# Spreading dt over the state partitions by DMA instead of by matmul, in stage 1 of a four-stage model

## The chip, the cores and the metric

The kernel runs on one core of a Trainium2 chip. The metric is the device time of one execution in microseconds; lower is better.

## What is computed

The input x has shape (2, 64, 64, 64) in float32. Four blocks are applied to it one after the other, each as `x = x + block(groupnorm(x))`. The first is a small graph and attention block, the third and fourth are Mamba2 blocks. The second, here called stage 1, is a selective state space block, and only it is changed. For each of 128 sequences of 64 steps, with 128 inner channels and 16 states for each channel, it computes (cut down from the reference):

```python
u  = silu(conv(x_in) + b_conv)
dt = softplus((u @ W_xproj[:4].T) @ W_dt.T + b_dt)
A  = -exp(A_log)
def step(h, (dt_t, B_t, C_t, u_t)):
    h = h * exp(dt_t[..., None] * A) + dt_t[..., None] * B_t[:, None, :] * u_t[..., None]
    y = einsum('bds,bs->bd', h, C_t)
```

Afterwards come y + u * D, a gate silu(z), the output projection and a layer norm.

## The kernel before

**Blocks and slots.** Stage 1 works through 16 blocks (`NK1`), each of 8 sequences of 64 steps, which is 512 columns. A tile has 128 partitions (inner channels) by 512 columns of float32, 256 KB. The recurrence needs channels times states, 2048 rows, so each block is cut into 16 slots (`S1`): slot s handles eight channels with all their 16 states, on 128 partitions. `channels_of(t)` gives the quarter q = s % 4 and the part r = s // 4, and the eight channels are the partitions 32q + 8r to 32q + 8r + 7 of the tile. There are 256 slots over the stage, counted by t.

**One slot.** Five steps follow each other, each on its own engine.

1. TensorE (`spread`, L539) copies the eight rows of dt (tile `dt1`) over the 128 partitions by a matmul with a 0/1 matrix, into PSUM bank 2 or 3. It does the same with the eight rows of dt * u (tile `dtu`) into bank 4, 5 or 6. Each is one float32 matmul from 32 rows, which appears in the trace as two weight loads and two matmuls. The two spreads of one turn of the loop lie in different quarters of the array.
2. ScalarE (L893) computes exp(dt * A) from the dt bank into one of three tiles `decay1`.
3. VectorE (`weigh`, L1345) multiplies the bank of dt * u by B, in place.
4. VectorE (`scan`, L1354) runs the recurrence over the columns into one of four tiles `hs`.
5. GpSimd (L1088) multiplies the result by C into one of eight tiles `hc`. After each four slots, TensorE (L564) gathers them back to channels in bank 7.

**The order.** Each engine runs a program written out by hand, slot by slot, in order, with waits on semaphores. In turn t TensorE spreads dt for slot t + 3, once the exponential of slot t + 1 is done, and dt * u for slot t + 2, once the scan of slot t - 1 is done; then it gathers, then it does its share of `front`. ScalarE computes the exponential of slot t + 2 once the scan of slot t - 1 is done. VectorE weighs slot t + 1 and scans slot t.

**The front.** While the slots of block k run, all engines prepare block k + 1 in small steps tied to the slot number (`front(s, f)`): the input projection in bank 0 (s = 0), u (s = 1), B and C (s = 2, 3), dt before the softplus in bank 0 and z in bank 1 (s = 3), the softplus (s = 5 to 11), and dt * u (s = 12). In the softplus ScalarE computes e = exp(-|v|) and the inverse of 2 + e into `inv1` (L867), VectorE multiplies them (L1338), and GpSimd adds the last term at L1065, which makes dt ("final"), and multiplies by u at L1070 ("ready"). Per block GpSimd does 16 multiplications for the slots and seven for the front and the gate.

**SyncE.** Its queue issues the kernel's loads at the start. From the end of stage 1 on it issues, for each of the eight later calls, transfers from SBUF to SBUF (`rows_of_x`, L358 and L359, from 64 partitions to 64), stores of 128 partitions to device memory (L363) and loads of rows into few partitions (`decay_rows` L253, `decay_cols` L261, the latter into three partitions at a time). During stage 1 it issues nothing.

Of the kernel before, what the change touches and what calls it, by code (L numbers as in the profile page):

```python
# [13 lines left out]
ALU = mybir.AluOpType  # L14
ACT = mybir.ActivationFunctionType
# [62 lines left out]
def program(nc, x, consts, pool_sel, state_sel, l0w, l1w, callw, out):  # L78
    ctx = ExitStack()
    with ctx:  # L80
# [220 lines left out]

            return (u - 3) % 8 in (7, 0, 3)

        U_BANKS, T_BANKS = (4, 5, 6), (2, 3)

        PARTS = {"s1_x_parts": ("tanh_x", "half_x", "gate_x"),
                 "s1_z_parts": ("tanh_z", "z_copied", "gate_z"),
# [27 lines left out]
        @block.sync  # L335
        def _(sp):
            sp.dma_start(cst, consts).then_inc(sg("constants_loaded"), 16)
            for b in range(NB):
                sp.dma_start(Otok[:, :, b, :], x_tok[b].rearrange("(t p) c -> p t c", p=128)).then_inc(
                    sg("x_loaded"), 16)  # L340
            sp.dma_start(w0, l0w).then_inc(sg("stage0_weights_loaded"), 16)
            sp.dma_start(poolS, pool_sel).then_inc(sg("stage0_weights_loaded"), 16)
            sp.dma_start(w1, l1w).then_inc(sg("stage1_weights_loaded"), 16)
            sp.dma_start(stateS, state_sel).then_inc(sg("stage1_weights_loaded"), 16)
            for d in range(2):
                sp.dma_start(raws[d], callw[d]).then_inc(sg(f"block_weights_loaded{d}"), 16)

            def call(m, n, d, c):

                def rows_of_x(g):  # L350
                    sp.wait_ge(sg("normed"), c * 8 + g + 1)
                    if g >= 2:
                        sp.wait_ge(sg("x_projected"), c * 16 + 2 * (g - 1))
                        sp.wait_ge(sg("bc_projected"), c * 8 + g - 1)
                    a = SEQS * g
                    for b in range(NB):
                        own, dst = XP[64 * b:64 * b + 64, :], XS[g % 2][b]
                        sp.dma_start(dst[0:64, :], own[:, a + 1:a + 1 + SEQS]).then_inc(sg(f"x_rows{g % 2}"), 16)  # L358
                        sp.dma_start(dst[64:128, :], own[:, a:a + SEQS]).then_inc(sg(f"x_rows{g % 2}"), 16)  # L359

                def keep(name):
                    sp.wait_ge(sg(f"split_{name}"), c + 1)
                    sp.dma_start(kept[NAMES.index(name)].rearrange("(p j) n -> p (j n)", j=3), SPLITS[name]).then_inc(  # L363
                        sg(f"stored_{name}"), 16)

                def rows_of_decay(g):
                    if g >= 2:
                        sp.wait_ge(sg("decay_logs"), c * L + 8 * (g - 1))
                    decay_rows(sp, g, 0, "M")
                    decay_cols(sp, g, 0, "M")  # L370
                    decay_cols(sp, g, 1, "G")
                    decay_rows(sp, g, 1, "C")

                rows_of_x(0)
                rows_of_x(1)
                sp.wait_ge(sg("zeroed"), 1)
                keep("M")
                keep("G")
                keep("C")
                sp.wait_ge(sg("stored_M"), (c + 1) * 16)  # L380
                decay_rows(sp, 0, 0, "M")
                decay_cols(sp, 0, 0, "M")
                sp.wait_ge(sg("stored_G"), (c + 1) * 16)
                decay_cols(sp, 0, 1, "G")
                sp.wait_ge(sg("stored_C"), (c + 1) * 16)
                rows_of_decay(1)
                for g in range(2, NGROUP):
                    rows_of_x(g)
                    rows_of_decay(g)
                if c + 2 < 8:  # L390
                    sp.wait_ge(sg(f"block_done{d}"), m * 2 + n + 1)
                    sp.dma_start(raws[d], callw[c + 2]).then_inc(sg(f"block_weights_loaded{d}"), 16)

            rounds(sp, lambda m: None, call, lambda m: None)
            for b in range(NB):
                sp.wait_ge(sg("out_turned"), 8)
                sp.dma_start(out_tok[b].rearrange("(t p) c -> p t c", p=128), Otok[:, :, b, :]).then_inc(
                    sg("output_stored"), 16)
            sp.wait_ge(sg("output_stored"), 32)
# [9 lines left out]
        def _(pe):  # L409
# [97 lines left out]
            def stage1():  # L507
# [5 lines left out]
                def front(s, f):  # L513
                    if s == 0:
                        pe.wait_ge(sg("s1_staged"), 4 * f + 4)
                        if f >= 1:
                            pe.wait_ge(sg("s1dt_act"), made("s1dt_act", "relu", f))
                        mm(bank[0], W1("winx_a"), st[:, :, 3:3 + L], start=True, stop=False)
                        mm(bank[0], W1("winx_b"), st[:, :, 1:1 + L], start=False, stop=True).then_inc(
                            sg("s1_front_x"), 1)  # L520
                    if s == 2:
                        pe.wait_ge(sg("s1_u"), f + 1)
                        mm(bank[0], W1("wb"), u1[f % 3], start=True, stop=True).then_inc(sg("s1_b"), 1)
                        if f == 0:
                            pe.wait_ge(sg("s1_product_kept"), 1)
                        if f >= 3:
                            pe.wait_ge(sg("s1_stored"), f - 2)
                        mm(bank[1], W1("wc"), u1[f % 3], start=True, stop=True).then_inc(sg("s1_c"), 1)
                    if s == 3:
                        pe.wait_ge(sg("s1_b_copied"), f + 1)  # L530
                        mm(bank[0], W1("wdtx"), u1[f % 3], start=True, stop=True).then_inc(sg("s1_dtp"), 1)
                        pe.wait_ge(sg("s1_c_copied"), f + 1)
                        mm(bank[1], W1("wz"), st[:, :, 3:3 + L], start=True, stop=True).then_inc(
                            sg("s1_front_z"), 1)
# [7 lines left out]
                def slot(t):  # L542

                    k, s = t // S1, t % S1
                    tt, tu, ta = t + 3, t + 2, t - 5
                    if tt < NK1 * S1:
                        if tt % S1 == 0:
                            pe.wait_ge(sg("s1dt_pool"), made("s1dt_pool", "final", tt // S1 + 1))
                        if tt >= 2:
                            pe.wait_ge(sg("s1_dA"), tt - 1)  # L550
                        spread(bank[T_BANKS[tt % 2]], dt1, tt).then_inc(sg("s1_dt_wide"), 1)
                    if 0 <= tu < NK1 * S1:
                        if tu % S1 == 0:
                            pe.wait_ge(sg("s1dt_pool"), made("s1dt_pool", "ready", tu // S1 + 1))
                        if tu >= 3:
                            pe.wait_ge(sg("s1_h"), tu - 2)
                        spread(bank[U_BANKS[tu % 3]], dtu, tu).then_inc(sg("s1_u_wide"), 1)
                    if 0 <= ta < NK1 * S1 and ta % QUAD == 0:
                        r = ta % S1 // QUAD
                        pe.wait_ge(sg("s1_hc"), ta + QUAD)  # L560
# [214 lines left out]
        def _(act):  # L775
# [50 lines left out]
            def front(s, f):  # L826
# [36 lines left out]
                if s == 6:  # L863
                    act.wait_ge(sg("s1dt_act"), made("s1dt_act", "e", f + 1))
                    A(inv1, e1, ACT.Ln, bias=C("two")).then_inc(sg("s1dt_act"), 1)
                    act.wait_ge(sg("s1dt_act"), made("s1dt_act", "log", f + 1))
                    A(inv1, inv1, ACT.Exp, scale=-1.0).then_inc(sg("s1dt_act"), 1)  # L867
                if s == 8:
                    act.wait_ge(sg("s1dt_ratio"), f + 1)
                    A(ratio_sq, ratio1, ACT.Square).then_inc(sg("s1dt_act"), 1)  # L870
# [13 lines left out]
            def slot(t_):  # L884
# [1 line left out]
                k, s = t_ // S1, t_ % S1  # L886
                te = t_ + 2
                if 0 <= te < NK1 * S1:
                    act.wait_ge(sg("s1_dt_wide"), te + 1)
                    if te >= 3:  # L890
                        act.wait_ge(sg("s1_h"), te - 2)
                    q, r = channels_of(te)
                    A(dA[te % 3][:, :, 1:L], bank[T_BANKS[te % 2]].rearrange("p (s l) -> p s l", l=L)[:, :, 1:L],  # L893
                      ACT.Exp, scale=negA[:, QUAD * q + r:QUAD * q + r + 1]).then_inc(sg("s1_dA"), 1)
                if next_front(t_) is not None:
                    front(s, next_front(t_))
# [141 lines left out]
        def _(pool):  # L1038
# [3 lines left out]
            def front(s, f):  # L1042
# [17 lines left out]
                if s == 11:  # L1060
                    pool.wait_ge(sg("s1dt_pool"), made("s1dt_pool", "log1", f + 1))
                    pool.wait_ge(sg("s1dt_act"), made("s1dt_act", "relu", f + 1))
                    if f >= 2:
                        pool.wait_ge(sg("s1_dt_wide"), S1 * (f - 1))
                    g.tensor_tensor(dt1[f % 2], relu1, log1, ALU.add).then_inc(sg("s1dt_pool"), 1)  # L1065
                if s == 12:
                    pool.wait_ge(sg("s1dt_pool"), made("s1dt_pool", "final", f + 1))
# [75 lines left out]
        def _(dve):  # L1143
# [188 lines left out]
            def front(s, f):  # L1332

                if s == 7:
                    dve.wait_ge(sg("s1dt_act"), made("s1dt_act", "exp", f + 1))
                    if f >= 1:
                        dve.wait_ge(sg("s1dt_pool"), made("s1dt_pool", "log1", f))
                    v.tensor_tensor(ratio1, e1, inv1, ALU.mult).then_inc(sg("s1dt_ratio"), 1)  # L1338

            def weigh(t_):  # L1340

                dve.wait_ge(sg("s1_u_wide"), t_ + 1)
                if t_ % S1 == 0:
                    dve.wait_ge(sg("s1_b_copied"), t_ // S1 + 1)
                v.tensor_tensor(bank[U_BANKS[t_ % 3]], b_rep[(t_ // S1) % 2], bank[U_BANKS[t_ % 3]], ALU.mult).then_inc(  # L1345
                    sg("s1_dbu"), 1)

            def scan(t_):
# [2 lines left out]
                dve.wait_ge(sg("s1_dA"), t_ + 1)  # L1351
                if t_ >= 4:
                    dve.wait_ge(sg("s1_hc"), t_ - 3)
                v.tensor_tensor_scan(hs[t_ % 4], decay1[t_ % 3], bank[U_BANKS[t_ % 3]], 0.0, ALU.mult, ALU.add).then_inc(  # L1354
                    sg("s1_h"), 1)

            def read_out(k):
# [396 lines left out]
```

## Time and profile before

| | |
|---|---|
| Median of three runs | 2502.19 us (2499.79 to 2518.25) |
| Profiled execution | 2495.65 us, span 2493.8 us |
| Time of the execution outside its span | 1.85 us |
| Busy: TensorE, VectorE, ScalarE, GpSimd | 85%, 63%, 64%, 49% of the span |
| Mean granted TensorE clock | 0.833 of full speed |
| First and last scan of the slots start at | 143.1 and 821.0 us |

Stage 1's slots fill about the third to the thirteenth of the profile's forty slices. A share over the whole span mixes four different stages, so the stage is read by itself.

### The profile page before, as it was taken

The numbers are of one execution on the slowest core, as the hardware profiler recorded it, in microseconds if no ns is written. First come the engines' busy times: TensorE is split into PE (matmuls) and PEld (weight loads), VectorE is DVE, ScalarE is ACT, GpSimd is POOL, SyncE is SP. The second block draws the span as 40 slices with busy tenths as digits, with TensorE's granted clock in tenths as the row PEclk, the third lists the DMA queues.
The fourth block names the chain that finished last, engine by engine and source line by source line (L and its number), as shares of the span: only waits on it lengthen the run. The fifth ranks groups of instructions, "written<-read, shape, count | busy, mean of one in ns | idle before, by whom it ended". The sixth has DMA issues, their size and how long they took to land.

```text
span 2493.8 us, 59585 instructions
## 1 busy us (share of the span) xinstructions
PE 2110.6 (85%) x24808; PEld 1011.8 (41%) x24808; DVE 1559.9 (63%) x2232; ACT 1588.9 (64%) x2571; POOL 1219.1 (49%) x970
## 2 busy tenths in 40 slices
PE   4379999999999679979979979967997997996996
PEld 3122222222222235535525535534553552553553
DVE  3457667676767666557656656656655665665663
ACT  1266556565654458757857857866775775785784
POOL 0056667666666526525606625623551660662563
PEclk7567566666766689989989989988988998998997
DMA  4000000000000021022012111102102201211111
GB/s 134 0 0 1 1 1 1 1 1 1 1 1 0 1 65 39 17 65 50 18 56 48 30 55 41 37 20 59 41 14 67 49 18 56 47 30 42 40 39 35
DMA packets 95517, 75.95 MB, mean 30 GB/s; under 512 B 65936, under 2 KB 74128, under 8 KB 94864
## 3 DMA queue, kind: packets, MB, share of 16 engines
q1 hardware_dynamic: 91984, 71.75, 11.6%
q8 instruction: 196, 3.21, 0.5%
q10 hardware_dynamic: 3264, 0.39, 0.1%
q14 instruction: 73, 0.60, 0.1%
HBM read 25.45 MB, written 11.53 MB: 15 GB/s over the span
## 4 chain that ended last, share of the span: by engine, by line
PE 56%; issue 11%; DVE 11%; ACT 11%; POOL 10%; DMA 1%; ACTq 0%; POOLq 0%; SPq 0%; DVEq 0%
PE bank L640 10%; PE bank L709 7%; PE bank L672 6%; PE bank L721 6%; PE bank L653 5%; PE bank L539 5%; POOL Z L1088 5%; PE bank L729 5%; ACT bank L996 3%; PE bank L624 2%; DVE XP L1414 2%; PE bank L564 2%; ACT SQ L964 1%; PE bank L635 1%; ACT O L992 1%
## 5 line engine op out<-in xcount | busy, mean ns | idle before, releaser
L1126 POOL TENSOR_TENSOR SQ<-SQ,folded_weights 128x512 f32<-128x512 f32 x192 | 244.1, 1274 | 674.7 <-DVE SQ L1525 674.7
L1088 POOL TENSOR_TENSOR Z<-Z,Y 128x512 f32<-128x512 f32 x256 | 323.4, 1266 | 201.1 <-DVE Z L1354 191.8
L539 PE MATMUL bank<-SS,Z 32*128 32x512 f32 x512 | 406.8, 913 | 0.4
L1354 DVE TENSOR_TENSOR_SCAN Z<-SS,bank 128x512 f32<-128x512 f32 x256 | 310.0, 1211 | 0.0
L1345 DVE TENSOR_TENSOR bank<-Y,bank 128x512 f32<-128x512 f32 x256 | 175.9, 687 | 195.9 <-PE bank L539 195.9
L1132 POOL TENSOR_TENSOR SQ<-O,SQ 128x512 f32<-128x512 f32 x208 | 264.8, 1275 | 63.9 <-ACT O L992 35.7
L893 ACT ACTIVATE SS<-bank,small 128x504 f32<-128x504 f32 x256 | 172.6, 676 | 182.0 <-PE bank L539 111.0
L640 PE MATMUL bank<-folded_weights,work 128*64 128x128 f32 x4096 | 285.8, 284 | 0.0
L672 PE MATMUL bank<-SS,work 32*128 32x512 bf16 x1024 | 209.5, 389 | 62.3 <-ACT bank L996 45.0
L709 PE MATMUL bank<-SQ,work 128*32 128x64 f32 x8192 | 259.1, 227 | 1.2 <-POOL SQ L1126 0.8
L640 PEld LDWEIGHTS bank<-folded_weights,work 128*64 128x64 f32 x4096 | 224.8, 139 | 78.9 <-issue 78.9
L1467 DVE SCALAR_TENSOR_TENSOR work<-SQ,bank 64x512 f32<-64x512 f32 x256 | 175.4, 685 | 109.0 <-ACT SQ L964 107.0
L709 PEld LDWEIGHTS bank<-SQ,work 128*32 128x32 f32 x8192 | 185.2, 114 | 83.9 <-issue 76.7
L653 PE MATMUL bank<-work,folded_weights 128*32 128x512 f32 x1024 | 138.2, 658 | 91.1 <-DVE XP L1414 91.1
L1545 DVE TENSOR_TENSOR bank<-bank,constants 128x512 f32<-128x512 f32 x192 | 133.5, 695 | 106.5 <-PE bank L672 105.9
L539 PE MATMUL bank<-work,Z 32*128 32x512 f32 x256 | 178.2, 976 | 17.3 <-ACT SS L893 13.3
L988 ACT ACTIVATE bank<-bank 128x512 f32<-128x512 f32 x192 | 112.8, 587 | 122.8 <-PE bank L672 122.8
L539 PE MATMUL bank<-SQ,Z 32*128 32x512 f32 x256 | 160.8, 911 | 33.9 <-POOL SQ L1065 17.8
L996 ACT ACTIVATE bank<-bank 128x512 f32<-128x512 f32 x320 | 189.3, 591 | 0.0
L709 PE MATMUL bank<-folded_weights,work 128*32 128x64 f32 x5120 | 182.2, 232 | 3.7 <-POOL SQ L1132 3.7
L992 ACT ACTIVATE O<-bank 128x512 f32<-128x512 f32 x208 | 124.4, 598 | 90.2 <-PE bank L672 81.5
L1475 DVE SCALAR_TENSOR_TENSOR Z<-bank,Z 128x512 f32<-128x512 f32 x128 | 88.5, 692 | 114.1 <-ACT bank L1009 112.4
(276 smaller groups left out, 3890.7 us busy)
## 6 DMA issues: line engine op xcount, KB each, us to landing
work<-XP SPq DMA_DIRECT2D x256, 134.0 KB, 2.4
decays_kept<-extra SPq DMA_DIRECT2D x24, 384.0 KB, 2.3
SS<-decays_kept SPq DMA_DIRECT2D x256, 24.0 KB
block_weights<-callw SPq DMA_DIRECT2D x8, 735.0 KB, 4.2
work<-decays_kept SPq DMA_DIRECT2D x240, 24.0 KB
out<-O SPq DMA_DIRECT2D x2, 1024.0 KB, 8.5
constants<-consts SPq DMA_DIRECT2D x1, 1453.5 KB, 6.2
Y<-l0w SPq DMA_DIRECT2D x1, 1156.0 KB, 10.2
```

The lines of the kernel that those rows point to most:

```text
L539: return mm(out, spread8[r][h, :], tile[(t // S1) % 2][h, :], start=True, stop=True, tile_position=(32 * q, 0))
L640: last = mm(bank[3][64 * b:64 * b + 64, 128 * j:128 * j + 128], XS[(k // 2) % 2][b][:, PADL * q + at:PADL * q + at + L], w, start=False, s ...
L653: last = mm(bank[6][32 * j:32 * j + 32, :], wbc[t][:, 32 * j:32 * j + 32], src, start=(t == 0), stop=(t == 1), tile_position=(0, 32 * j), ...
L672: return mm(bank[u % 3], LHS[r][h, 2 * a:2 * a + 128], cols[h, :, :], start=(k == 0), stop=(k == 1), tile_position=(32 * k, 0), skip_group ...
L709: last = mm(bank[4 + k % 2][32 * h4:32 * h4 + 32, a:a + 64], xs[:, 32 * h:32 * h + 32], by[:, 64 * h:64 * h + 64], start=first_ or multipl ...
L996: A(bank[u % 3], bank[u % 3], ACT.Abs).then_inc(sg("abs_by_act"), 1)
L1088: g.tensor_tensor(hc[t_ % 8], hs[t_ % 4], c_rep[k % 2], ALU.mult).then_inc(sg("s1_hc"), 1)
L1126: g.tensor_tensor(MM[u % 3], MM[u % 3], Dhalf, ALU.add).then_inc(sg("mixed"), 1)
L1132: g.tensor_tensor(MM[u % 3].rearrange("p (h l) -> p h l", l=L), DK[u % 3].rearrange("p (h l) -> p h l", l=L), GM[(u // 8) % 2][:, 64 * (u ...
L1345: v.tensor_tensor(bank[U_BANKS[t_ % 3]], b_rep[(t_ // S1) % 2], bank[U_BANKS[t_ % 3]], ALU.mult).then_inc(sg("s1_dbu"), 1)
L1354: v.tensor_tensor_scan(hs[t_ % 4], decay1[t_ % 3], bank[U_BANKS[t_ % 3]], 0.0, ALU.mult, ALU.add).then_inc(sg("s1_h"), 1)
L1467: last = v.scalar_tensor_tensor(X2[k % 2].rearrange("p (n b e) -> p n b e", b=2, e=HP)[h, :, b, :], TX[h, :].rearrange("p (n e) -> p n e", ...
```

## The change

Three things are done.

- dt is no longer spread by TensorE. SyncE issues one DMA for each slot, 256 in all. Each reads the slot's eight rows of `dt1`, each row sixteen times, and writes a tile `dt_wide` of 128 partitions by 512 columns in SBUF. There are four such tiles, in a part of `extra` that nothing uses in this stage. The DMA of slot t waits until the exponential of slot t - 4 is done. ScalarE reads the tile once its DMA has landed.
- The freed banks 2 and 3 go to dt * u, which now has five banks. TensorE spreads it for slot t + 3, once the scan of slot t - 2 is done (before: for slot t + 2, once the scan of slot t - 1 is done).
- The inverse in the softplus is written to PSUM bank 0 instead of back to `inv1`, and VectorE reads it there. TensorE writes the next block's projection into that bank only once VectorE has read it.

```diff
-        U_BANKS, T_BANKS = (4, 5, 6), (2, 3)
+        U_BANKS = (2, 3, 4, 5, 6)
+        dt_wide = [extra[:, 512 * i:512 * i + 512] for i in range(4)]
...
+            for t in range(NK1 * S1):
+                if t % S1 == 0:
+                    sp.wait_ge(sg("s1dt_pool"), made("s1dt_pool", "final", t // S1 + 1))
+                if t >= 4:
+                    sp.wait_ge(sg("s1_dA"), t - 3)
+                q, r = channels_of(t)
+                rows = dt1[t // S1 % 2][32 * q + 8 * r:32 * q + 8 * r + 8, :]
+                sp.dma_start(dt_wide[t % 4], rows.unsqueeze(1).broadcast_to([8, S1, 512])).then_inc(
+                    sg(f"s1_dt_wide{t % 4}"), 16)
...
-                            pe.wait_ge(sg("s1dt_act"), made("s1dt_act", "relu", f))
+                            pe.wait_ge(sg("s1dt_ratio"), f)
...
-                    tt, tu, ta = t + 3, t + 2, t - 5
-                    if tt < NK1 * S1:
-                        if tt % S1 == 0:
-                            pe.wait_ge(sg("s1dt_pool"), made("s1dt_pool", "final", tt // S1 + 1))
-                        if tt >= 2:
-                            pe.wait_ge(sg("s1_dA"), tt - 1)
-                        spread(bank[T_BANKS[tt % 2]], dt1, tt).then_inc(sg("s1_dt_wide"), 1)
+                    tu, ta = t + 3, t - 5
...
-                        if tu >= 3:
-                            pe.wait_ge(sg("s1_h"), tu - 2)
-                        spread(bank[U_BANKS[tu % 3]], dtu, tu).then_inc(sg("s1_u_wide"), 1)
+                        if tu >= 5:
+                            pe.wait_ge(sg("s1_h"), tu - 4)
+                        spread(bank[U_BANKS[tu % 5]], dtu, tu).then_inc(sg("s1_u_wide"), 1)
...
-                    A(inv1, inv1, ACT.Exp, scale=-1.0).then_inc(sg("s1dt_act"), 1)
+                    A(bank[0], inv1, ACT.Exp, scale=-1.0).then_inc(sg("s1dt_act"), 1)
...
-                    act.wait_ge(sg("s1_dt_wide"), te + 1)
+                    act.wait_ge(sg(f"s1_dt_wide{te % 4}"), (te // 4 + 1) * 16)
...
-                    A(dA[te % 3][:, :, 1:L], bank[T_BANKS[te % 2]].rearrange("p (s l) -> p s l", l=L)[:, :, 1:L],
+                    A(dA[te % 3][:, :, 1:L], dt_wide[te % 4].rearrange("p (s l) -> p s l", l=L)[:, :, 1:L],
...
                     if f >= 2:
-                        pool.wait_ge(sg("s1_dt_wide"), S1 * (f - 1))
+                        for i in range(4):
+                            pool.wait_ge(sg(f"s1_dt_wide{i}"), S1 // 4 * (f - 1) * 16)
...
-                    v.tensor_tensor(ratio1, e1, inv1, ALU.mult).then_inc(sg("s1dt_ratio"), 1)
+                    v.tensor_tensor(ratio1, e1, bank[0], ALU.mult).then_inc(sg("s1dt_ratio"), 1)
```

## Rows read from the trace of the kernel before

**Rows 1.** The page: busy shares, and TensorE, its clock and DMA in 40 slices.

```profile
PE 2110.6 (85%) x24808; PEld 1011.8 (41%) x24808; DVE 1559.9 (63%) x2232; ACT 1588.9 (64%) x2571; POOL 1219.1 (49%) x970
...
PE   4379999999999679979979979967997997996996
...
PEclk7567566666766689989989989988988998998997
DMA  4000000000000021022012111102102201211111
```

**Rows 2.** The stretch of the slots: window, length, busy by engine, clock, DMA share, GB/s.

```profile
137.50:823.00 685.50, 643.98 (x1768) 197.32 (x1768) 482.53 (x542) 403.14 (x627) 450.66 (x362) 0.67 0.00 1
```

**Rows 3.** Groups of instructions, 139.3 to 821 us: busy, mean ns, idle before.

```profile
L539 PE MATMUL bank<-SS,Z 32*128 32x512 f32 x512 | 406.8, 913 | 0.4
L1088 POOL TENSOR_TENSOR Z<-Z,Y 128x512 f32<-128x512 f32 x254 | 320.9, 1266 | 200.7 <-DVE Z L1354 191.8 <-PE bank L564 8.8
L1354 DVE TENSOR_TENSOR_SCAN Z<-SS,bank 128x512 f32<-128x512 f32 x256 | 310.0, 1211 | 0.0
...
L1345 DVE TENSOR_TENSOR bank<-Y,bank 128x512 f32<-128x512 f32 x256 | 175.9, 687 | 195.9 <-PE bank L539 195.9
L893 ACT ACTIVATE SS<-bank,small 128x504 f32<-128x504 f32 x256 | 172.6, 676 | 182.0 <-PE bank L539 111.0 <-DVE Z L1354 70.9
```

**Rows 4.** The timeline of VectorE's scans, two slots running without a wait.

```profile
403.40 1.21 DVE L1354 TENSOR_TENSOR_SCAN Z<-SS,bank 128x512 f32<-128x512 f32 x1
...
405.11 1.21 DVE L1354 TENSOR_TENSOR_SCAN Z<-SS,bank 128x512 f32<-128x512 f32 x1
```

**Rows 5.** One line's instructions, the softplus product: duration min/median/max, first and last start.

```profile
L1338 DVE TENSOR_TENSOR SS<-SS x16: 692/1248/1252, 129.4 to 764.5; 128x512 f32<-128x512 f32 x16
```

**Rows 6.** The timeline of TensorE: spreads in a pair, one alone, a gather.

```profile
430.50 1.22 PE L539 MATMUL bank<-SQ,Z 32*128 32x512 f32 x1
...
430.51 1.22 PE L539 MATMUL bank<-SS,Z 32*128 32x512 f32 x1
...
434.53 2.07 PE L539 MATMUL bank<-SS,Z 32*128 32x512 f32 x2
...
439.10 1.93 PE L564 MATMUL bank<-Z 128*32 128x512 f32 x8
```

**Rows 7.** SyncE's timeline: one such issue, and four of 24 KB into three partitions.

```profile
1078.55 0.60 SPq L359 DMA_DIRECT2D work<-XP  x1
...
1092.81 1.42 SPq L261 DMA_DIRECT2D SS<-decays_kept  x4
```

**Rows 8.** DMA issues of the page: from SBUF to SBUF, KB each, us to landing.

```profile
work<-XP SPq DMA_DIRECT2D x256, 134.0 KB, 2.4
```

**Rows 9.** Windows in which transfers out of all 128 partitions (L363) run.

```profile
1089.00:1090.00 1.00, 0.00 (x0) 0.00 (x0) 0.96 (x3) 0.67 (x2) 0.00 (x0) 0.50 0.99 390
1090.00:1091.00 1.00, 0.00 (x0) 0.00 (x0) 1.00 (x2) 0.45 (x1) 0.00 (x0) 0.50 1.00 393
```

**Rows 10.** Windows in which transfers from 64 partitions to 64 run.

```profile
1078.00:1079.00 1.00, 1.00 (x4) 0.39 (x3) 0.93 (x3) 0.74 (x2) 0.00 (x0) 1.00 0.97 212
...
1080.00:1081.00 1.00, 1.00 (x4) 0.41 (x3) 0.97 (x2) 0.74 (x2) 0.00 (x0) 1.00 0.96 221
```

**Rows 11.** A window in which transfers into few partitions (L253, L261) run.

```profile
1093.00:1098.00 5.00, 5.00 (x35) 1.67 (x29) 0.00 (x0) 1.51 (x2) 0.00 (x0) 0.58 0.21 47
```

**Rows 12.** The timeline at the first dt and at the last scans.

```profile
136.14 1.26 POOL L1065 TENSOR_TENSOR SQ<-work 128x512 f32<-128x512 f32 x1
...
819.86 2.32 DVE L1354 TENSOR_TENSOR_SCAN Z<-SS,bank 128x512 f32<-128x512 f32 x2
```

More of the change, by code:

```diff
@@ L1344, in weigh @@
                     dve.wait_ge(sg("s1_b_copied"), t_ // S1 + 1)
-                v.tensor_tensor(bank[U_BANKS[t_ % 3]], b_rep[(t_ // S1) % 2], bank[U_BANKS[t_ % 3]], ALU.mult).then_inc(
+                v.tensor_tensor(bank[U_BANKS[t_ % 5]], b_rep[(t_ // S1) % 2], bank[U_BANKS[t_ % 5]], ALU.mult).then_inc(
                     sg("s1_dbu"), 1)
@@ L1353, in scan @@
                     dve.wait_ge(sg("s1_hc"), t_ - 3)
-                v.tensor_tensor_scan(hs[t_ % 4], decay1[t_ % 3], bank[U_BANKS[t_ % 3]], 0.0, ALU.mult, ALU.add).then_inc(
+                v.tensor_tensor_scan(hs[t_ % 4], decay1[t_ % 3], bank[U_BANKS[t_ % 5]], 0.0, ALU.mult, ALU.add).then_inc(
                     sg("s1_h"), 1)
```

## The prediction

> **What bounds the kernel now.** I read the page's slices first: the slots of stage 1 fill the slices in which TensorE is nearly always busy and its clock stands at 0.5 to 0.7 [rows 1]. The window of that stretch says the same: of 685.5 us TensorE is busy 644, VectorE 483, GpSimd 451, ScalarE 403, the granted clock is 0.67 (a mixture of 1.2 and 2.4 GHz), and DMA does nothing [rows 2]. The groups of the stretch then show who waits for whom [rows 3]. VectorE waits 195.9 us, always ahead of the weighing and always for a spread; ScalarE waits 111.0 us for a spread; GpSimd waits for the scans. So 685.5/256 = 2.68 us go by for a slot, where scans that don't wait start 405.11 - 403.40 = 1.71 us apart [rows 4]. A block takes (764.5 - 129.4)/15 = 42.3 us [rows 5]. The stage is set by TensorE's spreads, in alternation with VectorE. How the others stand: GpSimd has 23 multiplications for a block, 23 x 1.27 = 29.2 us; VectorE 16 x 1.71 and two of about 0.7, 28.8 us.
>
> **The change, part by part.**
>
> *dt's spreads leave TensorE.* 256 spreads go. But a spread of dt runs beside one of dt * u in another quarter: a matmul of each starts at 430.50 and 430.51, and a spread alone, at the low clock, still takes 2.07 us [rows 6]. Removing the partner shortens a lone pair by nothing. What it gives at most is VectorE's whole wait, 196 us. I price it in the fast rival below; in my forecast TensorE is no longer the bound.
>
> *Five banks for dt * u.* The spread is released by a scan one slot earlier and may run three slots ahead. It costs nothing and can only take from the same 196 us. The gathers, 1.93 us [rows 6], stay.
>
> *Inverse in PSUM.* The product at L1338 takes 1248 ns in the median and 692 at its shortest [rows 5]; the weighing, which also has one operand in PSUM, takes 687 [rows 3]. So up to 16 x 0.56 = 9 us of VectorE's time go. Bank 0 is held some two slots longer, from the third step of slot 5 to slot 7, and is next wanted in slot 0 of the next block: no cost. Both are hidden where VectorE waits for something else. I take nothing.
>
> *256 DMAs on SyncE.* An issue takes 0.60 us [rows 7], 154 us in all, on a queue that is empty in this stretch; the next transfers (L358) come after the stage, when the last of these has been issued. Cover: a slot of 1.7 us or more. Nothing.
>
> *The transfers themselves.* Each DMA writes 128 rows of 2048 bytes, 262,144 bytes, all read from eight partitions. Four may be in flight. Latency isn't the matter: a transfer from SBUF to SBUF lands 2.4 us after its issue [rows 8], and with four tiles 2.4/4 = 0.6 us for a slot. The matter is the rate, for which no row reads so few partitions. The nearest: out of 128 partitions 390 and 393 GB/s at a DMA share of 0.99 and 1.00 [rows 9]; from 64 to 64 partitions 212 and 221 GB/s at 0.97 and 0.96 [rows 10]. In the second the engines are just as occupied and move half as much, so what holds them is the number of partitions that they touch, not the engines. Bounds: at the full rate 262,144/392,000 = 0.67 us for a DMA; in proportion to the partitions read, 8/128 of 392 GB/s = 24.5 GB/s, 10.7 us. Small groups needn't be proportional: while rows go into three partitions at a time and into 24, DMA moves 47 GB/s [rows 11], and the four issues of 24 KB into three partitions come in 1.42 us, 69 GB/s [rows 7]. These rows are nearest in the number of partitions. They give 5.6 us and 3.8 us for a DMA. I take 54 GB/s, between them: **4.85 us for a DMA**.
>
> No row reads eight partitions, but a page has a price. The Trainium skill, "SBUF — State Buffer", section "Door 1: The DMA port swizzle", says that the bandwidth of a DMA goes by how many of 16 ports its partitions reach, 27.2 GB/s each, four neighbouring partitions to a port. Eight rows from a multiple of eight then lie in two ports: 54.4 GB/s, an estimate of 4.8 us for a DMA, and by that the sum would be some 10 us below mine. That 64 partitions move half of what 128 do agrees with it.
>
> *The wait added.* ScalarE now waits for the DMA ahead of each exponential. Queued behind it are its own steps of the front; the scan waits for the exponential, GpSimd for the scan, TensorE's next spread for the scan. At 4.85 us a slot a block takes 78 us, so ScalarE, GpSimd (29.2) and TensorE (about 40 now) all fit inside, even if TensorE falls to 1.2 GHz throughout. dt of the next block is final at slot 11, with four DMAs queued, so no gap arises between blocks.
>
> **The sum.** The first dt is final at 136.14 + 1.26 = 137.4 us [rows 12]. The first DMA follows; 1.8 us of fixed time (2.4 less 134.0/216 = 0.6) [rows 8, 10] and 256 x 4.85 = 1241.6 us later the last one lands, at 1380.8. One exponential (0.68) [rows 3] and the last scan starts at 1381.6. Now it starts at 819.86 + 2.32 - 1.21 = 821.0 [rows 12]. What follows is untouched. So 1381.6 - 821.0 = +560.6 us. Against the profiled execution, 2495.65 us, that is 3056; the median of the runs lies 6.5 us above it, so I forecast **3060 us**. By 69 GB/s (3.8 us) it would be 2790, by 47 GB/s (5.6 us) 3250. That is this case's own range.
>
> **The rivals.**
>
> *The transfers keep up* (faster). If a DMA takes under 2.68 us, the point from which this decides, so above 98 GB/s, all of them are hidden, and the gain of the first two parts appears. For it: repeated reads of a row might not be bound like reads of many rows, and rows of three partitions show no slowing that I can see. Against it: the halved rate in [rows 10]. The time: at most 196 us of VectorE's waits, at least nothing. GpSimd's 29.2 us for a block allows 15 x (42.3 - 29.2) = 196 us as well. TensorE's lone spreads and the front's matmuls keep part of it; I take half, 98 us: 2400 us. A rule of the Trainium skill would bring this about: "DMA: Bandwidth & Descriptors", section "Where 436 GB/s comes from", puts transfers inside SBUF at the fabric's 435 GB/s. By it a DMA would take an estimated 0.6 us; [rows 9] agree for 128 partitions, [rows 10] don't.
>
> *The transfers keep up, but TensorE still sets the pace* (no change). 16 lone spreads of 2.07 us and four gathers of 1.93 us [rows 6] are 40.8 us for a block, against 42.3 now, if spreads don't overlap each other and half the spreads are not enough to hold the clock at 0.67. Five banks let neighbours in different quarters overlap, which speaks against it. The time: 2495 us.
>
> *In between.* A DMA takes 2.7 to 3.8 us: 2500 to 2790.
>
> *One path only.* Eight neighbouring rows are read in proportion to their number, 10.7 us for a DMA: 256 x (10.7 - 4.85) = 1498 us more, 4550 us. For it: the strict halving between [rows 9] and [rows 10].
>
> **How the numbers follow.** The rate near 54 GB/s: 0.70, since the one row that varies the partitions shows the limit, and nothing shows it lifted. Keeping up with a gain: 0.17. Keeping up without: 0.05. In between: 0.03. One path: 0.05. A change under 1% can't be told from none here. So faster 0.17, same 0.05, slower 0.78. The likeliest case's own range is 2790 to 3250. To leave out no more than 2 in 10, the range goes down over the case in between to no change: 2480 to 3250.
>
> **What the profile after would show.** If right: slices 3 to 20 or so with a DMA busy share far above 0 and about 54 GB/s; a DMA landing 15 to 20 us after its issue, since three are ahead of it; the exponential at L893's place waiting for a DMA nearly every time, some 4 us; scans 4.85 us apart; VectorE's wait for spreads gone; TensorE's clock near 0.5, without harm. If the transfers keep up: landing within 4 us, the exponential waiting for scans, slots of 2.0 to 2.5 us. The inverse's part shows as 0.69 us for the product at L1338 in either case. What would make the forecast wrong: a rate from eight partitions that isn't within 47 to 69 GB/s.

## The result and the profile after

The changed kernel takes 2685.41 us in the median of four runs (2676.16 to 2691.35), the kernel before beside it 2501.03 us (2499.79 to 2518.25). The ratio is 1.0717, 95% interval 1.0658 to 1.0776: **slower by 7%**. The direction is the one forecast, the size isn't: +184 us where +561 were worked out. The time lies within the stated 2480 to 3250, but below the likeliest case's own 2790 to 3250. The profiled execution took 2680.60 us.

The page of the changed kernel, TensorE, its clock and DMA in 40 slices of 67 us, answers to [rows 1]:

```profile
PE 2015.6 (75%) x24296; PEld 957.0 (36%) x24296; DVE 1557.4 (58%) x2232; ACT 1604.7 (60%) x2571; POOL 1218.8 (45%) x970
...
PE   4346666667656665897897997996898898898896
...
PEclk6566666655556757898998998998898998898997
DMA  3044444444444440211211111111211211210211
GB/s 125 0 66 76 76 83 79 77 81 77 67 73 82 84 85 17 56 39 29 56 39 41 44 39 47 41 36 29 56 37 31 56 39 29 56 39 18 56 39 33
```

The stretch of the slots, as a window (busy times by engine, clock, DMA share, GB/s), answers to [rows 2]:

```profile
137.50:1010.00 872.50, 550.00 (x1264) 142.75 (x1264) 479.95 (x542) 417.93 (x627) 451.06 (x363) 0.62 0.46 77
```

The work of VectorE, ScalarE and GpSimd is what it was, TensorE's is 94 us less, and the stretch is 187 us longer: that is the whole difference. DMA moves 77 GB/s in it, at a share of 0.46. The groups of that stretch answer to [rows 3]:

```profile
L1094 POOL TENSOR_TENSOR Z<-Z,Y 128x512 f32<-128x512 f32 x256 | 322.9, 1267 | 259.2 <-DVE Z L1360 251.9 <-PE bank L569 7.1
L1360 DVE TENSOR_TENSOR_SCAN Z<-SS,bank 128x512 f32<-128x512 f32 x256 | 311.7, 1218 | 234.9 <-issue 163.8 <-DVE bank L1351 40.4 <-ACT SS L898 28.5
L550 PE MATMUL bank<-SS,Z 32*128 32x512 f32 x512 | 310.8, 916 | 176.5 <-POOL SS L1076 123.4 <-DVE Z L1360 52.8
L898 ACT ACTIVATE SS<-extra,small 128x504 f32<-128x504 f32 x256 | 182.7, 714 | 381.3 <-DMA extra<-work 192.2 <-DMA extra<-SQ 188.4
L1351 DVE TENSOR_TENSOR bank<-Y,bank 128x512 f32<-128x512 f32 x256 | 174.1, 680 | 119.5 <-PE bank L550 119.2
```

VectorE's waits for spreads fell from 195.9 to 119.2 us. They aren't gone, as was forecast, but the transfers set the pace: DMA never rests in the stretch. ScalarE waits 380.6 us (192.2 and 188.4) for DMAs ahead of its exponential, and the scan waits for ScalarE. The 163.8 us put down to "issue" are such waits wherever the timeline was read: the third exponential below ends at 318.02, and the scan starts at 318.10. The timeline of ScalarE shows how they come (start, length, and what the wait ended on), with that scan last:

```profile
309.87 0.72 ACT L898 ACTIVATE SS<-extra,small 128x504 f32<-128x504 f32 x1 [3.58 <-DMA extra<-SQ]
312.13 0.72 ACT L898 ACTIVATE SS<-extra,small 128x504 f32<-128x504 f32 x1 [1.53 <-DMA extra<-SQ]
317.30 0.72 ACT L898 ACTIVATE SS<-extra,small 128x504 f32<-128x504 f32 x1 [3.80 <-DMA extra<-work]
319.69 0.72 ACT L898 ACTIVATE SS<-extra,small 128x504 f32<-128x504 f32 x1 [1.02 <-DMA extra<-work]
...
318.10 1.22 DVE L1360 TENSOR_TENSOR_SCAN Z<-SS,bank 128x512 f32<-128x512 f32 x1 [3.36 <-issue]
```

They come in pairs: two DMAs within 2.3 us, then a gap of 5. Scans are (1006.2 - 146.3)/255 = 3.37 us apart in the mean, where 2.66 were before and 4.85 were forecast. This line has the start of the first and of the last:

```profile
L1360 DVE TENSOR_TENSOR_SCAN Z<-SS,bank x256: 1208/1221/1222, 146.3 to 1006.2; 128x512 f32<-128x512 f32 x128
```

### The profile page after: what moved, and what is told of

Same layout as the page of the kernel before. It is cut to its first block, busy times and chain, and to the rows that moved or that the text cites. A ratio compares the mean times of both kernels' runs of the same rounds, so it can differ in the third digit from the quotient of the medians.

```text
span 2678.8 us, 58845 instructions
## 1 busy us (share of the span) xinstructions
PE 2015.6 (75%) x24296; PEld 957.0 (36%) x24296; DVE 1557.4 (58%) x2232; ACT 1604.7 (60%) x2571; POOL 1218.8 (45%) x970
## 4 chain that ended last, share of the span: by engine, by line
PE 44%; DMA 13%; issue 10%; ACT 10%; DVE 8%; POOL 6%; ACTq 0%; POOLq 0%; SPq 0%; DVEq 0%
PE bank L645 10%; DMA extra<-work 8%; PE bank L714 6%; PE bank L677 6%; PE bank L726 5%; PE bank L658 5%; DMA extra<-SQ 5%; PE bank L734 4%; POOL Z L1094 3%; ACT bank L1001 3%; PE bank L629 2%; DVE XP L1420 2%; PE bank L640 1%; ACT SQ L969 1%; ACT O L997 1%
## 5 line engine op out<-in xcount | busy, mean ns | idle before, releaser
L1360 DVE TENSOR_TENSOR_SCAN Z<-SS,bank 128x512 f32<-128x512 f32 x256 | 311.7, 1218 | 234.9 <-issue 163.8
L550 PE MATMUL bank<-SS,Z 32*128 32x512 f32 x512 | 310.8, 916 | 176.5 <-POOL SS L1076 123.4
L898 ACT ACTIVATE SS<-extra,small 128x504 f32<-128x504 f32 x256 | 182.7, 714 | 381.3 <-DMA extra<-work 192.2
L1351 DVE TENSOR_TENSOR bank<-Y,bank 128x512 f32<-128x512 f32 x256 | 174.1, 680 | 119.5 <-PE bank L550 119.2
L550 PEld LDWEIGHTS bank<-SS,Z 32*128 32x128 f32 x512 | 81.7, 255 | 403.9 <-DVE Z L1360 154.4
L1138 POOL TENSOR_TENSOR SQ<-SQ 128x512 f32<-128x512 f32 x112 | 142.8, 1275 | 34.1 <-ACT SQ L997 23.0
```

Source lines behind the costliest of these rows:

```text
L550: return mm(out, spread8[r][h, :], tile[(t // S1) % 2][h, :], start=True, stop=True, tile_position=(32 * q, 0))
L898: A(dA[te % 3][:, :, 1:L], dt_wide[te % 4].rearrange("p (s l) -> p s l", l=L)[:, :, 1:L], ACT.Exp, scale=negA[:, QUAD * q + r:QUAD * q + r ...
L1138: g.tensor_tensor(MM[u % 3].rearrange("p (h l) -> p h l", l=L), DK[u % 3].rearrange("p (h l) -> p h l", l=L), GM[(u // 8) % 2][:, 64 * (u ...
```

## The experiments

Three theories were tested. **P**: a few neighbouring source rows share one path, and DMAs in flight from other rows can use other paths beside it. **E**: the engines that serve a DMA of this shape are the bound, whatever it reads. **L**: four tiles are too few for the time to landing. Times are medians beside the kernel before on the same chip: 2495 us for the first four kernels, 2497 for the next four, 2493 for the last four. The kernels with the same rows, full width, four groups in turn and one in flight were run once each.

**The same rows each time.** The changed kernel with one source address for all DMAs.

```diff
-                rows = dt1[t // S1 % 2][32 * q + 8 * r:32 * q + 8 * r + 8, :]
+                rows = dt1[t // S1 % 2][0:8, :]
```

> All 256 DMAs read rows 0 to 7 of the dt tile, whatever the slot (so dt is that of the wrong channels from the second slot on); bytes, pieces, waits and the sixteenfold reading are as in the changed kernel. Theory P (a few neighbouring source rows share one path of about 27 GB/s, eight rows lie on two, and the changed kernel reached 81 GB/s because the DMAs in flight read from different paths): now no two DMAs can use different paths, 54 GB/s, 4.85 us for a DMA, total about 2495 + 560 = 3060 us (2990 to 3100). Theory E (the engines that a DMA of this shape uses are the bound, whatever rows they read): 2685 us. Theory L (four tiles are too few for the time to landing): 2685 us.

Measured: 3206 us, above the 2990 to 3100 expected: the price of one DMA is 5.35 us (262,144 bytes at 49 GB/s), not 4.85. The scans are (1525.2 - 145.9)/255 = 5.41 us apart. The DMA view of 300 to 340 us in forty slices of 1 us, first of this kernel:

```profile
DMA  4444444444444444444454444444444444444444
GB/s 49 49 47 47 49 49 49 49 45 49 49 49 47 49 49 49 47 49 49 47 66 49 55 51 47 49 49 49 47 47 49 49 49 49 49 49 45 49 49 49
```

Then of the changed kernel:

```profile
DMA  4444344444444444444444444544444444433454
GB/s 49 49 109 115 86 59 53 51 47 96 104 92 53 49 53 47 70 125 109 61 49 53 66 119 111 94 70 51 76 119 107 96 76 55 117 104 72 98 86 47
```

Nothing differs but the address of the source, and one stream is flat at 49 GB/s, while the other swings between 49 and about 110 in a period of some 7 us, the time of two DMAs. E and L, which expected 2685 us, fall. 49 GB/s is two sixteenths of the 392 GB/s of [rows 9], and the engines are as occupied (0.46) as at the 86 GB/s of the next-but-one experiment.

**Rows four apart.** The same computation, with the channels of a slot chosen otherwise:

```diff
-                rows = dt1[t // S1 % 2][32 * q + 8 * r:32 * q + 8 * r + 8, :]
+                rows = dt1[t // S1 % 2][32 * q + r:32 * q + 32:4, :]
...
-        state[:, 128 * r:128 * r + 128] = (p % 32)[:, None] == (8 * r + p // 16)[None, :]
-        state[:, 512 + 32 * r:544 + 32 * r] = (8 * r + p // 16)[:, None] == np.arange(32)[None, :]
+        state[:, 128 * r:128 * r + 128] = (p % 32)[:, None] == (r + 4 * (p // 16))[None, :]
+        state[:, 512 + 32 * r:544 + 32 * r] = (r + 4 * (p // 16))[:, None] == np.arange(32)[None, :]
...
-    g["alog"] = w["A_log"].reshape(16, 8, 16).transpose(1, 2, 0).reshape(128, 16)
+    g["alog"] = w["A_log"].reshape(4, 8, 4, 16).transpose(1, 3, 0, 2).reshape(128, 16)
```

> A slot takes the channels 32q + r + 4i (i = 0 to 7) in place of 32q + 8r + i, and the matrices for spreading and gathering and the table of A are permuted to fit, so the result is the same computation. Each DMA still reads eight rows sixteen times each, but they lie four partitions apart. 
Measured: 2457.7 us, ratio to the kernel before 0.9829 (0.9784 to 0.9873). P holds, and this form is **faster than the kernel before**, by 1.3 to 2.2%. The DMA view of 300 to 340 us:

```profile
DMA  5555555555555545200455202500435552151000
GB/s 184 139 135 139 137 141 143 137 139 137 139 139 143 147 115 168 78 12 0 182 143 137 61 8 113 150 0 0 176 86 186 137 135 66 59 170 33 0 0 0
```

With the same number of rows, each read sixteen times, DMA moves about 140 GB/s while it works, and it comes to rest in between, which it never does in the two views above. That is 1.9 us for a DMA, not the 1.3 to 1.5 expected, and still under the slot. Why it isn't eight sixteenths of 392 GB/s, 196, wasn't tested.

**The quarters in turn.** The order of the quarters in four slots is 0, 2, 1, 3; the gather is fitted to it.

```diff
-            return s % QUAD, s // QUAD
+            return (0, 2, 1, 3)[s % QUAD], s // QUAD
...
```

> The order of the quarters within four slots is 0, 2, 1, 3 in place of 0, 1, 2, 3, so that DMAs that follow each other read from the lower and the upper 64 partitions in turn; everything else and the result stay. Theory P: two paths more are open to nearly every pair of DMAs, 81 GB/s goes up towards 107, 2.5 to 2.9 us for a DMA, total 2500 to 2600 us. Theory E and theory L: no difference, 2685 us.

Measured: 2594.8 us, ratio 1.0355 (1.0290 to 1.0420), 90 us less than the changed kernel. The time is within the range expected, the rate isn't: 86 GB/s, 3.05 us for a DMA, where 2.5 to 2.9 were expected. The window of 300 to 700 us, of this kernel and then of the changed one:

```profile
300.00:700.00 400.00, 260.54 (x643) 69.40 (x644) 242.72 (x278) 218.65 (x335) 232.03 (x187) 0.67 0.46 86
```

```profile
300.00:700.00 400.00, 255.81 (x587) 66.86 (x590) 222.60 (x253) 197.42 (x297) 213.41 (x172) 0.61 0.46 78
```

The DMA share is the same, the bytes aren't. In the changed kernel quarters 0 and 1 read from the lower 64 partitions, 2 and 3 from the upper, and for equal r the first two read from places 32 apart; those pairs don't help each other, which is the swing above. ScalarE's timeline of the changed kernel bears it out. Where two exponentials in a row waited for a DMA, that of quarter 1 starts 2.58 us after that of quarter 0, and that of 3 as long after that of 2, but from 1 to 2 it takes 4.39 us, and from 3 to the next 0 4.66 (medians of 29 to 39 cases each). The exponentials at 309.87 and 312.13 are those of quarters 2 and 3. From 305 to 309 us, ahead of them, DMA moves 53 GB/s, though the next quarter 0 has been issued since 304.30; from 309 to 312, as quarter 2 lands and 3 after it, it moves 98. So the next group seems to join only when the first of a pair is nearly done.

**Full width.** Each DMA copies all 128 rows; what arrives isn't the slot's dt.

```diff
-                sp.dma_start(dt_wide[t % 4], rows.unsqueeze(1).broadcast_to([8, S1, 512])).then_inc(
+                sp.dma_start(dt_wide[t % 4], dt1[t // S1 % 2]).then_inc(
```

> Each DMA copies the whole dt tile, 128 rows to 128 partitions, without repetition (so what arrives isn't the slot's dt): the same bytes written, from all partitions. Theories P and E: about 390 GB/s, 0.7 us for a DMA, hidden under the slot; the time shows what the rest of the change is worth, about 2400 us (2340 to 2490). Theory L: a landing of 2.3 us in place of more than ten, also fast.

Measured: 2454.4 us. Rows four apart (2457.7) are about as good as the full width; the transfer is no longer what binds. So the rest of the change is worth about 40 us, not the 98 of the fast rival.

**Three banks again**, on top of rows four apart:

```diff
-        U_BANKS = (2, 3, 4, 5, 6)
+        U_BANKS = (4, 5, 6)
...
-                    tu, ta = t + 3, t - 5
+                    tu, ta = t + 2, t - 5
...
-                        if tu >= 5:
-                            pe.wait_ge(sg("s1_h"), tu - 4)
+                        if tu >= 3:
+                            pe.wait_ge(sg("s1_h"), tu - 2)
```

> On top of e2_strided (2458 us), the five banks for dt*u are undone: three banks, spread for slot t + 2 once the scan of slot t - 1 is done, as before the change. Theory B (the gain of e2_strided over the kernel before comes from the banks, which let TensorE run ahead of VectorE): 2480 to 2500 us. Theory S (it comes from the 256 spreads that TensorE no longer does): 2450 to 2465 us.

Measured: 2491.7 us in the median of ten runs (2474.9 to 2501.0), ratio 0.9940 (0.9904 to 0.9977). By the interval the 256 spreads removed, with the inverse in PSUM, give 6 to 24 us alone, 15 in the middle. The interval doesn't meet that of rows four apart, so the two banks that the spreads free add to it: by the middles of the intervals, 0.6% of 1.7% come without them. The window of 300 to 700 us, with three banks and then with five:

```profile
300.00:700.00 400.00, 342.62 (x776) 87.72 (x774) 290.09 (x333) 259.64 (x402) 280.96 (x226) 0.66 0.36 102
```

```profile
300.00:700.00 400.00, 291.89 (x796) 76.45 (x796) 281.89 (x330) 259.17 (x400) 276.49 (x224) 0.76 0.36 104
```

With five banks TensorE is busy for less of the time and the granted clock is higher, 0.76 against 0.66. VectorE waits 147.0 us for spreads where it waits 196.0 with three (139 to 850 us). How much of this is TensorE running ahead and how much the clock, these runs don't separate.

**Inverse back in SBUF**, on top of rows four apart: `A(inv1, inv1, ...)` and `e1, inv1`, and TensorE's wait with them, as before the change.

> On top of e2_strided (2458 us), the inverse of the softplus goes back to SBUF, and TensorE waits for the relu again instead of the product. If 0.56 us of VectorE in each of 16 blocks counts: 2467 us. If it is hidden behind VectorE's waits for spreads: 2458 us, within the runs' spread.

Measured: 2466.7 us (2460.7 to 2482.2), ratio 0.9882 (0.9828 to 0.9937). The interval overlaps that of rows four apart, so whether this part counts stays open. Its stated reason doesn't hold here, as the product's line shows:

```profile
L1344 DVE TENSOR_TENSOR SS<-SS x16: 691/692/693, 129.6 to 737.4; 128x512 f32<-128x512 f32 x16
```

With both operands in SBUF it takes 692 ns, not the 1248 of [rows 5]. In the new order of events it is short either way.

**Earlier steps on GpSimd**, on top of rows four apart: in `front`, `s == 10` becomes 9, `s == 11` and `s == 12` become 10.

> On top of e2_strided, GpSimd does the last three steps that make dt and dt*u of the next block one to two slots earlier (slots 9, 10, 10 in place of 10, 11, 12); nothing else moves. Theory G (what is left in stage 1 is the turn of the block: TensorE waits 208 us in all for dt*u of the next block, ScalarE for the first DMAs, VectorE for the first spreads, some 3.5 us in each of 15 blocks): about 40 us less, 2405 to 2430 us. Theory C (GpSimd and VectorE are now close to full, so earlier front steps only delay GpSimd's products for the slots): 2450 to 2480 us.

Measured: 2436.0 us (2421.0 to 2447.3), ratio 0.9737 (0.9669 to 0.9804): the lowest ratio of all, 2.0 to 3.3% under the kernel before; its interval still touches that of rows four apart (0.9784 to 0.9873). From 180 to 780 us TensorE's weight loads wait 77.2 us for the next block's dt * u in place of 115.8, and VectorE 106.6 us for spreads in place of 130.6. The 2405 to 2430 us of theory G were missed by 6 us.

**Four groups in turn.** The changed kernel with q and r exchanged in the row address.

> The changed kernel's DMAs, still of eight adjacent rows read sixteen times each, but with q and r of the row address exchanged, so that four DMAs in a row read from four different groups of eight rows (dt is then that of the wrong channels). Theory P with overlap (one DMA alone is held at 49 GB/s by its two paths, and the rate over that comes only from DMAs in flight on other paths): the rate rises above e3_alternate's 87 GB/s, to 100 to 150 GB/s, total 2460 to 2550 us. If the eight engines march in step through the queue (no overlap), each DMA takes 5.35 us as in e1_same_rows and the total is about 3200 us. Theory E (adjacency within a DMA matters, the neighbours in the queue don't): 2685 us.

Measured: 2591.8 us, and in the window:

```profile
300.00:700.00 400.00, 270.84 (x662) 72.92 (x662) 244.60 (x279) 222.73 (x342) 235.76 (x190) 0.67 0.47 88
```

88 GB/s, no more than with quarters in turn, where 100 at least were expected. The total, too, lies above the 2460 to 2550 expected. Neighbours in the queue do matter, but four different groups are no better than two. What holds the overlap at 88 GB/s isn't shown. That the engines take their DMAs in order, and so are mostly in the same rows, would fit what was seen from 305 to 309 us, but it was not tried by itself.

**One in flight.**

```diff
+                if t >= 1:
+                    sp.wait_ge(sg(f"s1_dt_wide{(t - 1) % 4}"), ((t - 1) // 4 + 1) * 16)
```

> The changed kernel, but SyncE issues each DMA only once the one before it has landed. Theory P with overlap (a DMA alone moves 49 GB/s as in e1_same_rows, and the changed kernel's 81 GB/s comes from two DMAs in flight on different paths): 5.35 us of transfer and some 1.8 us fixed, 7.1 us for a slot, a landing of 7 us, total 2501 + 256 x (7.1 - 2.66) = 3640 us. If a single DMA already moves 81 GB/s: 3.2 + 1.8 = 5.0 us for a slot, 3100 us.

Measured: 3622.9 us, close to the 3640 expected with overlap. This is the changed kernel, with its own rows, and it moves in bursts of one DMA each; 300 to 330 us in slices of 0.75 us:

```profile
DMA  0444444300254444410144454430034444440014
GB/s 11 55 44 52 49 49 46 41 14 0 35 52 44 49 52 52 44 22 0 16 49 49 49 52 46 46 41 0 0 44 52 49 49 46 46 52 11 0 25 52
```

49 GB/s in each burst, a scan each (1947.5 - 145.1)/255 = 7.07 us: 5.35 of transfer and 1.7 fixed. So a DMA by itself costs what the same-rows kernel showed, and the changed kernel's 78 GB/s are overlap.

**The kernel before, with GpSimd's steps earlier.** The same edit of `front` on the kernel before.

> The kernel before the change, with only GpSimd's last steps for dt and dt*u moved one to two slots earlier, as in e8_front_earlier. If the turn of the block is as dear there: 2475 us, so that 20 us of e8_front_earlier's gain need no DMA. If TensorE's spreads hide it there (its spreads come one slot later than in the changed order): 2497 us.

Measured: 2470.4 us, ratio 0.9901 (0.9872 to 0.9931). That is the case in which the turn of the block is as dear there. So 0.7 to 1.3% can be had with this edit and no DMA at all, of the 2.6% of the best kernel.

**All steps earlier**, on top of GpSimd's: VectorE's product at slot 6, ScalarE's squares at slot 7, GpSimd's at 8, 8, 9, 9.

> On top of e8_front_earlier (2436 us), the softplus steps from VectorE's product on are one slot earlier on VectorE, ScalarE and GpSimd. If TensorE's remaining 132 us of waits for the next block's dt*u and ScalarE's for the first DMAs still cost something: 2415 to 2430 us. If the steps then wait for each other and hold up the slots behind them: 2436 to 2460 us.

Measured: 2444.8, 2494.3, 2507.4 and 2507.7 us. These runs lie too far apart for a comparison, and the lowest is above the 2436.0 us of GpSimd's steps alone. Nothing shows a gain from the further steps.

**Five tiles** for dt in the changed kernel, so that five DMAs may be in flight.

```diff
-                if t >= 4:
-                    sp.wait_ge(sg("s1_dA"), t - 3)
+                if t >= 5:
+                    sp.wait_ge(sg("s1_dA"), t - 4)
...
```

> The changed kernel with five tiles for dt in place of four, so that five DMAs may be in flight. Theory P: the rate is what binds, a fifth DMA lets a little more overlap; 2640 to 2685 us. Theory L (too few tiles for the time to landing): a fifth more slots in the same time, 3.37 x 4/5 = 2.7 us for a slot, 2510 us.

Measured: 2716.4 us, ratio 1.0893 (1.0852 to 1.0934). L is refuted: more in flight gives nothing. That it is 31 us slower than four tiles, none of the theories says, and P's 2640 to 2685 us were missed as well; the rate fell from 78 to 75 GB/s from 300 to 700 us. Why is left open. One stretch of its trace bears on E once more, the last number but one being the DMA share:

```profile
306.00:307.00 1.00, 0.00 (x0) 0.00 (x0) 1.00 (x2) 0.20 (x1) 1.00 (x2) 0.50 0.24 49
```

From 305 to 309 us half the usual engines are at work, at 0.24, and DMA still moves the 49 GB/s of the same-rows kernel at 0.46. So the engines aren't what holds it.

## Why the prediction was right and wrong

**What binds: right.** The transfers' rate, limited by the source partitions and not by issue, latency or engines, became the bound, and ScalarE's exponential is where it shows. The same-rows kernel and the one with one DMA in flight both move 49 GB/s, inside the 47 to 69 of [rows 11] and [rows 7]. That is partly luck. Those rows are loads from device memory (`decays_kept`), where few partitions are written and none read, and the 69 is the pace of four issues on the queue, not of bytes. With one in flight the issue takes 607 ns and the fixed part is 1.7 us, much as priced. The prediction took the number of partitions touched as the limit. It is which ones: eight neighbours give 49 GB/s, eight rows four apart about 140.

**The size: wrong, in the sum.** The step that failed is "256 x 4.85 us later the last one lands". It took the price of one DMA, 4.85 us (5.35 as measured), and multiplied it by all 256, as if the four in flight read from the same place each time. They don't: q and r move the rows. The slots came 3.37 us apart, 256 x (4.85 - 3.37) = 379 us less than forecast. With 5.35 us the same sum would have come out 128 us higher still. The code shows in `channels_of` that the address changes from slot to slot; that DMAs from different rows overlap, no row of before showed, but the sum put the overlap at nothing without a reason. The time is that of the case "in between", given 0.03, though not by its mechanism: a DMA doesn't take 2.7 to 3.8 us, several share the time. The chances left outside the range, 0.17 and 0.05, are also a little more than the 2 in 10 named.

**The page.** The Trainium skill, "SBUF — State Buffer", section "Door 1: The DMA port swizzle", gives four neighbouring partitions to a port, and the partition 32 further to the same one. By it eight neighbours lie on two ports and eight rows four apart on eight, and slots of quarters 0 and 1 share two ports, those of 2 and 3 two others. The traces agree, with 49 against 140 GB/s for the first and with the pace in pairs of the exponentials for the second. Its 27.2 GB/s for a port is 24.5 here (49/2). It was used for one DMA alone. The section doesn't say that DMAs in flight on different ports add up; the 78 to 88 GB/s against 49 of these runs show it.

**One path only (10.7 us): no.** Reading in proportion to the rows would have given 24.5 GB/s for a DMA; it is 49.

**The transfers keep up: right as a mechanism, too large.** At rows four apart the gain is 40 us, not 98. It was taken as half of VectorE's 196 us of waits. Of them 147 remain there, all ahead of the weighing and for TensorE. Part of that is the block's turn: with GpSimd's steps earlier, 24 us of them go (130.6 to 106.6 from 180 to 780 us). And by the middles of the intervals the larger part of the gain came with the banks, which were priced at nothing of their own. [rows 9], which the prediction sets beside transfers inside SBUF, go to device memory, so they price none inside SBUF.

**The inverse: right to take nothing**, though for another reason than the cover named: in the new order the product takes 692 ns with both operands in SBUF too. **VectorE's wait for spreads** was to be gone; 119.2 us of it stay, while DMA doesn't rest.

**TensorE's clock.** "Near 0.5" was expected; it is 0.61 in 300 to 700 us, without harm as the transfers set the pace. It is 0.58 in the same-rows kernel.

## What to carry to other kernels

Price a DMA that reads or writes few partitions by which partitions they are, and then price the queue: here DMAs in flight overlapped only where they read from other groups. Where a slot may choose its rows freely, take them four apart rather than adjacent; another row address and the constant tables permuted to fit made the difference between 7% slower and 2% faster. And ask what the freed resource (here two PSUM banks) is worth apart from the freed work.

## What the runs showed of the hardware

- DMA out of eight adjacent partitions moves 49 GB/s, from eight partitions four apart about 140 GB/s, all of it to 128 partitions of SBUF; out of 128 partitions to device memory it is 392 GB/s [rows 9].
- The DMA share doesn't tell the rates apart: 0.46 at 49, 78, 86 and (0.47) 88 GB/s, and 0.24 at 49 with half the engines. Engines held up at the source count as busy, so a share far above what the GB/s need (the full-width kernel moves 103 GB/s at 0.28) is the sign of a narrow source.
- DMAs in flight from different groups of eight rows add up, as far as 78 to 88 GB/s where one alone moves 49.
- The share of 0.46 is near eight of sixteen engines. The Trainium skill, "DMA: Bandwidth & Descriptors", section "Why a DMA increments its semaphore by 16 and not by 1", says that a DMA runs on the largest number of engines, at most 16, that divides the slowest dimension of both its sides. For eight rows read and 128 written that is eight; the trace agrees.
